# Queries' chain ahead of the first context's normalisation, and a last layer in one block

## The chip, the cores and the metric

One core of a Trainium2 chip runs the whole program. The metric is the device time of one execution in microseconds (us), median of several runs. All data are float32.

## What is computed

The reference is a stack of four levels, L0 to L3. Each level adds to the latents `x` (8 batches x 64 tokens x 256 features) a cross-attention with a context of 8 x 1601 tokens, a self-attention or state-space layer, and a feed-forward layer with experts. Each layer sees the layer-normalised `x`. Two of the twelve layers matter here.

The first, L0's cross-attention, with 16 heads of 64 features:

```
ctx' = layernorm(ctx) * ln_x_g + ln_x_b
lat  = layernorm(layernorm(x)) * ln_l_g + ln_l_b
q = rmsnorm(lat @ Wq) * qn_g ;  k, v = split([ctx'; lat] @ Wkv) ;  k = rmsnorm(k) * kn_g
x = x + softmax(q k' / 8 + mask) v @ Wout + bout
```

The last, L3's feed-forward layer, works on one normalised input z of 512 tokens x 256:

```
q, k, v = z @ W_qkv + b_qkv            # 16 heads of 16, 8 batches of 64 tokens
att = softmax(q k' / 4) v
gate = softmax(z @ W_gate + b_gate) ;  combine = the two largest of 8 entries, others 0
moe = sum over e of combine[:, e] * (z @ W_experts[e] + b_experts[e])
x = x + att + moe
```

The attention and the experts read the same z. Neither needs the other's result.

## The kernel before

The code issues every engine's instructions itself. An engine runs its own queue in order, and the queues meet only at semaphores. A layer is one block; `end_layer` (line 519) ends it with a barrier of all engines. `x` lives in SBUF as `L.x` (128 partitions, 4 tiles of 256), z as `L.z`, its transpose as `L.zT`. `program` (line 3932) loads x, constants and the first layer's weights on SyncE's queue (SP), then for each layer opens a small block in which SP issues the next layer's weights (lines 3954 to 3957), and then runs the layer. The weights alternate between `weights_a` and `weights_b`.

**L0's cross-attention (`l0_xattn`, line 770).** 64 steps, 8 batches x 8 head pairs. Ahead of the steps lie two preparations.

- The queries' chain. TensorE (PE) projects 8 parts with `project_q` (line 1262). ScalarE (ACT) squares each (1172), PE takes the mean per head with `mean_q` (1270), VectorE (DVE) clamps it (1005), ACT takes Ln and Exp (1163, 1165), and DVE multiplies (996, `q_gained`). With four PSUM banks, `project_q(p)` for p of 4 or more waits for the `q_gained(p - 4)` of four parts before, and `mean_q(p)` waits for the clamp of part p - 2.
- The first context. SP loads it into `keys_tok`. DVE takes statistics of two pieces of seven tiles each (`ctx_stats`: 950, 955, 958), ACT makes 1/std (`ctx_rstd`: 1156, 1158), DVE subtracts and multiplies tile by tile (`ctx_norm`: 965), and GpSimd (POOL) applies gain and bias for each piece (1126, 1128, `gains`), and then makes the mask row (1136).

DVE's queue has, in this order: both `ctx_stats`, both `ctx_norm`, and then the eight clamps with their gains. ACT's queue has both `ctx_rstd` ahead of its first square. PE's first work behind the queries, `turn_keys` (1296), waits for all eight queries, for POOL's last gain and bias, and for two copies of latents (`move_latents`). From there on the 64 steps follow.

**L3's last layer (`l3_ffn`, line 3809).** Two calls, two blocks. The first is `self_attention` (222). It normalises x, projects V (440) and Q, K (447), takes scores (457) and copies them out (325). Then come, for each of four tiles t: `shift` (329, 330), Exp on ACT (400), `divide` (336 to 338), a turn of the probabilities on PE (465, `turn_probs`), its copy by ACT (404), their product with V (476, `weigh`), `even_heads` on ACT (414), `attended` on DVE (345), a turn back (486, `project`) and `residual` (352). PE has dummy products in its gaps (`keep_busy`, 204). The second is `experts` (2625). Its logits (2845) go through `gate_vector` (2582 to 2622, a chain of small DVE operations with one Exp on ACT), two copies (2738, 2739), a turn of the combine matrix (2863) and its copy (2742). Then a loop over 8 experts:

```
pe.wait_ge(y_taken, e)      # PE: 16 products into the one pair of result banks (2901)
dve.wait_ge(y_done, e + 1)  # DVE: x += result * combine, four tiles (2774)
last.then_inc(y_taken, 1)
```

After the loop PE multiplies the biases (2913) and DVE adds them (2789). The last block stores x (3962).

## Time and profile before

| | before |
|---|---|
| median of 3 runs | 3238.86 us (3234.41 to 3239.84) |
| the profiled execution | 3242.19 us, of which the span from first to last instruction is 3240.4 us |
| granted TensorE clock, mean | 0.938 |
| instructions | 43628 |
| start of L0's step loop's preparation (`turn_keys`) | 69.73 us |
| last layer's first instruction to x's last addition | 3122.82 to 3235.93 us |

Times are those of one profiled execution, counted from its first instruction. The busy shares are averages over twelve layers with different limits, so the two places of the change are read on their own: us 0 to 70, and us 3122 to the end.

### The profile page before, as it was taken

What the parts mean: (1) busy time and instruction counts of PE and PEld (TensorE: products, weight loads), DVE (VectorE), ACT (ScalarE), POOL (GpSimd) and SP (SyncE); (2) the same over time, 40 slices, a digit from 0 to 9 for tenths busy, and PEclk for the clock granted to TensorE, in tenths of its full rate; (3) what the DMA queues carried; (4) which work ended last, traced back from release to release, by engine and by line L of the source; (5) the groups of instructions that cost most, each with busy time, mean ns of one, the idle gap of its engine ahead of it and who ended that gap; (6) DMA issues with size and microseconds to landing.
All of it is one profiled execution on the core that took longest, in us unless ns stands there. A gap on an engine that the chain in (4) does not pass through costs nothing. (4 is left out here: it accounts for less than half of the span.)

```text
span 3240.4 us, 43628 instructions
## 1 busy us (share of the span) xinstructions
PE 2822.7 (87%) x17456; PEld 1910.0 (59%) x17456; DVE 1634.3 (50%) x3626; ACT 1088.7 (34%) x1925; POOL 522.3 (16%) x280
## 2 busy tenths in 40 slices
PE   5899999999999998789999779989955789588776
PEld 2566666666666665446565536657932559477644
DVE  5556565665646454445555357754520520355463
ACT  2333333333333331135555446622311613111120
POOL 2012020211202000000000007731010320243200
PEclk8899999999999999889999989999977889799888
DMA  4123323232322210311000001126856158332101
GB/s 139 45 53 73 69 55 66 54 66 54 66 59 61 54 44 23 145 45 42 21 21 22 1 16 40 43 84 243 301 191 203 50 193 306 131 122 82 32 1 33
DMA packets 92096, 271.40 MB, mean 84 GB/s; under 512 B 7920, under 2 KB 57096, under 8 KB 85240
## 3 DMA queue, kind: packets, MB, share of 16 engines
q1 hardware_dynamic: 87896, 259.65, 26.6%
q0 software_dynamic: 2976, 8.13, 0.7%
q8 instruction: 138, 2.26, 0.3%
q10 hardware_dynamic: 1024, 0.86, 0.1%
q14 instruction: 62, 0.51, 0.1%
HBM read 256.64 MB, written 11.44 MB: 83 GB/s over the span
## 5 line engine op out<-in xcount | busy, mean ns | idle before, releaser
L1375 PE MATMUL L_xattn_bank<-L_xattn_keys_tok,L_xattn_probsT 119*128 119x257 f32 (+1 forms) x1792 | 452.7, 393 | 9.3 <-ACT L_xattn_probsT L1211 0.4
L1312 PE MATMUL L_xattn_wide<-L_xattn_keys_feat,weights_a 128*128 128x512 f32 (+2 forms) x1024 | 386.4, 521 | 1.3 <-DVE L_xattn_k_rnorm L1024 0.7
L1375 PEld LDWEIGHTS L_xattn_bank<-L_xattn_keys_tok,L_xattn_probsT 119*128 119x128 f32 (+1 forms) x1792 | 320.9, 190 | 96.5 <-issue 33.1
L1312 PEld LDWEIGHTS L_xattn_wide<-L_xattn_keys_feat,weights_a 128*128 128x128 f32 x1024 | 192.0, 193 | 153.8 <-issue 127.7
L1020 DVE COPY L_xattn_k_normed<-L_xattn_wide 128x833 f32<-128x833 f32 (+1 forms) x128 | 131.3, 1026 | 231.2 <-PE L_xattn_wide L1312 231.2
L2315 DVE TENSOR_TENSOR_SCAN L_attn_state<-L_attn_decay,L_attn_banks 128x1024 f32<-128x1024 f32 x80 | 182.7, 2286 | 69.6 <-PE L_attn_banks L2518 61.6
L1590 DVE CUSTOM_DVE_ANT_0 L_xattn_scores<-L_xattn_banks,L_xattn_mask 128x512 f32<-128x512 f32 (+1 forms) x256 | 131.4, 570 | 151.8 <-issue 151.8
L2421 POOL TENSOR_TENSOR L_attn_state<-L_attn_state,L_attn_C_rows 128x1024 f32<-128x1024 f32 x80 | 188.7, 2360 | 70.3 <-DVE L_attn_state L2315 70.2
L1126 POOL TENSOR_TENSOR L_xattn_keys_tok<-L_xattn_keys_tok,weights_a 119x1792 f32<-119x1792 f32 (+2 forms) x24 | 61.1, 2546 | 856.1 <-DVE L_xattn_keys_tok L965 856.1
L1205 ACT ACTIVATE L_xattn_scores<-L_xattn_scores,L_xattn_neg_max 128x833 f32<-128x833 f32 x128 | 119.6, 982 | 208.6 <-DVE L_xattn_neg_max L1045 208.6
L2518 PEld LDWEIGHTS L_attn_banks<-L_attn_B_diagonal,L_attn_dt_u_tok 128*128 128x128 f32 x1280 | 150.4, 193 | 66.3 <-issue 64.7
L1040 DVE CUSTOM_DVE_ANT_0 L_xattn_scores<-L_xattn_wide,L_xattn_mask_row 128x833 f32<-128x833 f32 x128 | 126.4, 1021 | 110.2 <-issue 110.2
L1656 ACT ACTIVATE L_xattn_probsT<-L_xattn_banks 128x512 f32<-128x512 f32 (+1 forms) x208 | 122.6, 597 | 163.7 <-PE L_xattn_banks L1728 163.7
L3407 PE MATMUL L_ffn_banks<-L_ffn_slot_features,L_ffn_expert_w 128*128 128x128 f32 x1440 | 169.1, 278 | 3.0 <-DVE x_tok L3237 3.0
L1211 ACT ACTIVATE L_xattn_probsT<-L_xattn_bank 119x512 f32<-119x512 f32 x128 | 76.4, 597 | 276.5 <-PE L_xattn_bank L1352 276.5
L2518 PE MATMUL L_attn_banks<-L_attn_B_diagonal,L_attn_dt_u_tok 128*128 128x128 f32 x1280 | 165.2, 283 | 3.9 <-ACT L_attn_B_diagonal L2377 3.9
L3407 PEld LDWEIGHTS L_ffn_banks<-L_ffn_slot_features,L_ffn_expert_w 128*128 128x128 f32 x1440 | 166.3, 195 | 3.8 <-DVE x_tok L3237 3.7
L1030 DVE TENSOR_TENSOR L_xattn_k_normed<-L_xattn_k_scale,L_xattn_k_normed 128x834 f32<-128x834 f32 x128 | 155.6, 1257 | 0.8 <-DMA L_xattn_k_scale<-L_xattn_k_scale_rows 0.8
L1728 PE MATMUL L_xattn_banks<-const,L_xattn_scores 128*128 128x128 f32 (+1 forms) x832 | 134.2, 288 | 24.7 <-DVE L_xattn_V L1581 10.7
L2056 PE MATMUL L_xattn_banks<-L_xattn_ctx_tok_and_one,L_xattn_k_tok 128*128 128x257 f32 (+1 forms) x416 | 108.5, 416 | 31.6 <-ACT L_xattn_k_by_ctx L2012 29.5
L1728 PEld LDWEIGHTS L_xattn_banks<-const,L_xattn_scores 128*128 128x128 f32 (+1 forms) x832 | 88.8, 142 | 79.3 <-issue 45.8
L1664 ACT ACTIVATE L_xattn_scores<-L_xattn_scores,L_xattn_neg_max 128x1601 f32<-128x1601 f32 x64 | 103.5, 1618 | 92.7 <-DVE L_xattn_neg_max L1593 92.7
(504 smaller groups left out, 4562.6 us busy)
## 6 DMA issues: line engine op xcount, KB each, us to landing
L_xattn_k_scale<-L_xattn_k_scale_rows SPq DMA_DIRECT2D x128, 417.0 KB, 5.1
L_xattn_ctx_feat<-in_ctx_feat SPq DMA_DIRECT2D x24, 1601.0 KB, 10.0
L_ffn_expert_w<-in_x_L_ffn SPq DMA_DIRECT2D x16, 2056.0 KB, 8.0
L_ffn_expert_w<-in_x_L_ffn SPq DMA_DIRECT2D x15, 1028.0 KB, 6.2
L_ffn_expert_w<-in_x_L_ffn SPq DMA_DIRECT2D x15, 1024.0 KB, 5.2
L_attn_C_rows<-L_attn_c_rows SPq DMA_DIRECT2D x48, 256.0 KB, 3.2
L_xattn_ctx_tok<-in_ctx_tok SPq DMA_DIRECT2D x8, 1536.0 KB
L_xattn_ctx_tok_and_one<-in_ctx_tok SPq DMA_DIRECT2D x8, 1536.0 KB
```

The lines of the kernel that those rows point to most:

```text
L1020: nc.vector.tensor_copy(kn[:, s % 2, a:a + n], ps).then_inc(k_copied, 1)
L1030: nc.vector.tensor_tensor(k, spread[:, 2 * x:2 * x + 2, :], k, ALU.mult).then_inc(kn_ready, 1)
L1040: nc.vector.tensor_tensor_reduce(sc2[:, h, 0:HALF], ps, mrow[b % 2][:, :], 1.0, -3.0e38, ALU.add, ALU.max, mx[:, h:h + 1]).then_inc(s_take ...
L1312: last = nc.tensor.matmul(wide[:, 2 * h + c, 0:n], wk[:, k, p * P:(p + 1) * P], xnT[b % 2][:, k, a:a + n], start=(k == 0), stop=(k == KT - 1))
L1375: last = nc.tensor.matmul(bS[:, 0:D + 1], pT[0:r, c, a, :, :].rearrange("p h q -> p (h q)"), xn[b % 2][0:r, t, :], start=(i == 0), stop=(i ...
L1590: nc.vector.tensor_tensor_reduce(sc[:, j, a:a + n], ps[:, j, 0:n], mk[:, a:a + n], 1.0, -3.0e38, ALU.add, ALU.max, mx[:, j, c:c + 1]).then ...
L1656: nc.scalar.activation(pT[0:r, i % RING, :, :], ps[0:r, 6 + n % 2, :].rearrange("p (a n) -> p a n", n=P), ACT.Copy).then_inc(pT_ready, 1)
L1728: last = nc.tensor.transpose(ps[0:r, 6 + n % 2, j * P:(j + 1) * P], sc[:, j, t * P:t * P + r], L.ident)
L2315: nc.vector.tensor_tensor_scan(h[:, p % RING, :, :].rearrange("p m n -> p (m n)"), dA[:, p % RING, :, :].rearrange("p m n -> p (m n)"), ba ...
L2421: nc.gpsimd.tensor_tensor(state, state, C[:, g % C_RING, :].unsqueeze(1) .broadcast_to([P, 2, N]), ALU.mult).then_inc(hC_ready, 1)
L2518: last = nc.tensor.matmul(banks[:, i + j, t * P:(t + 1) * P], duT[d][:, t, m * P:(m + 1) * P], diag[:, g % DIAG_RING, t, :], start=True, s ...
L3407: last = nc.tensor.matmul(bank[:, c, :], w1[:, k, f:f + P], xT[:, j % 2, k, :], start=(k == 0), stop=(k == KT - 1))
```

## The change

It has three parts.

1. In `l0_xattn` the queries' chain comes ahead on DVE and ACT. The two `ctx_stats` now stand behind the clamps and gains of parts 1 and 2, and the two `ctx_norm` behind those of parts 3 and 4. On ACT `ctx_rstd` stands behind parts 2 and 3.
2. The first layer has no small block ahead of it any more. SP issues the second layer's weights inside `l0_xattn`, behind the first context, its mask and both copies of latents, ahead of the second context.
3. `l3_ffn` calls one new function, `attention_and_experts`, in place of `self_attention` and `experts`. All eight experts' weights are loaded by two transfers at the layer's start. PE's dummy products are gone; the experts' products stand between the attention's steps, written out by hand. The results of an expert go to one of two pairs of banks, ACT scales them into `expert_out`, POOL adds them up in `experts_total`, and one addition on DVE adds the total to x at the end. The scores' four tiles share four banks, so the second pair of tiles is computed after the first pair has been copied out. The expert biases go into the bank of the attention's `project` as one more product. `experts` is deleted; nothing else called it.

The diff, cut to its core:

```
+def attention_and_experts(L, nc, w, w_ready, at):
...
+        def s_view(t):
+            c = (t % 2) * 256
+            return ps[:, 0:4, c:c + 256].rearrange("p j (a s) -> p j a s", s=S)
...
+        def o_view(t, h, k):
+            return ps[:, 2 * (t % 2):2 * (t % 2) + 2, (2 * h + k) * S:(2 * h + k + 1) * S]
+        def y_view(e):
+            return ps[:, 4 + 2 * (e % 2):6 + 2 * (e % 2), :].rearrange("p a (t n) -> p (a t) n", n=D)
+        with nc.Block() as block:
+            @block.sync
+            def _(sp):
+                for n in range(2):
+                    sp.dma_start(we[:, 4 * n:4 * n + 4, :], src[4 * n:4 * n + 4].rearrange("e p c -> p e c")
+                                 ).then_inc(experts_loaded[n], 16)
+            @block.vector
+            def _(dve):
...
+                norm_vector(L, dve, chain, ln_stats_ready, rstd_ready, z_ready)
...
+                    last = nc.vector.tensor_scalar(hb[:, m, :], hs[:, :], w[:, bq + m:bq + m + 1], None, ALU.mult)
+                chain(last)
+                nc.vector.tensor_copy(half[:, 0, 0, 0:2], hs[:, :]).then_inc(hs_ready, 1)
+                dve.wait_ge(zT_turned, 1)
+                nc.vector.tensor_copy(L.zT[:, 1, :], ps[:, 1, :]).then_inc(zT_ready, 1)
+                dve.wait_ge(logits_ready, 1)
+                gate_vector(L, nc, dve, chain, T, ps[:, 0, 0:NT * E], w[:, at["br"]:at["br"] + E], "top2", None,
+                            logits_taken, gate_exp_ready)
+                nc.vector.tensor_copy(half[:, 0, 0, 0:2], comb[:, 0, 0:2]).then_inc(comb_ready, 1)
+                dve.wait_ge(combT_turned, 1)
+                nc.vector.tensor_copy(combT[:, :, :], ps[0:E, 1, :].rearrange("p (t n) -> p t n", n=P)
+                                      ).then_inc(combT_ready, 1)
...
+                def residual(t):
+                    dve.wait_ge(projected, t + 1)
+                    nc.vector.tensor_tensor(L.x[:, t, :], L.x[:, t, :], ps[:, 2 * (t % 2), 0:D], ALU.add
+                                            ).then_inc(x_added, 1)
...
+                residual(3)
+                dve.wait_ge(x_added, NT)
+                dve.wait_ge(y_added, E)
+                chain(nc.vector.tensor_tensor(L.x[:, :, :], L.x[:, :, :], total[:, :, :], ALU.add))
+            @block.gpsimd
+            def _(pool):
+                for e in range(E):
+                    pool.wait_ge(y_scaled, e + 1)
+                    if e == 0:
+                        nc.gpsimd.tensor_copy(total[:, :, :], ys[0][:, :, :]).then_inc(y_added, 1)
+                    else:
+                        pool.wait_ge(y_added, e)
+                        nc.gpsimd.tensor_tensor(total[:, :, :], total[:, :, :], ys[e % 2][:, :, :], ALU.add).then_inc(y_added, 1)
+            @block.scalar
+            def _(act):
...
+                nc.scalar.activation(L.zT[:, 0, :], ps[:, 0, :], ACT.Copy).then_inc(zT_ready, 1)
+                act.wait_ge(logits_taken, 1)
...
+                def scale_expert(e):
+                    act.wait_ge(y_done, e + 1)
+                    if e == 0:
+                        act.wait_ge(comb_ready, 1)
+                    if e >= 2:
+                        act.wait_ge(y_added, e - 1)
+                    for t in range(NT):
+                        last = nc.scalar.activation(ys[e % 2][:, t, :], y_view(e)[:, t, :], ACT.Copy,
+                                                    scale=comb[:, t, e:e + 1])
+                    last.then_inc(y_scaled, 1)
+                scale_expert(0)
+                exponentials(0)
+                exponentials(1)
+                scale_expert(1)
+                scale_expert(2)
+                copy_turned(0)
+                exponentials(2)
+                even_heads(0)
+                copy_turned(1)
+                exponentials(3)
+                scale_expert(3)
+                even_heads(1)
+                scale_expert(4)
+                copy_turned(2)
+                scale_expert(5)
+                even_heads(2)
+                copy_turned(3)
+                scale_expert(6)
+                even_heads(3)
+                scale_expert(7)
+            @block.tensor
+            def _(pe):
...
+                pe.wait_ge(zT_ready, 2)
+                for t in range(NT):
+                    for k in range(KT):
+                        last = nc.tensor.matmul(ps[:, 0, t * E:(t + 1) * E], L.zT[:, k, t * P:(t + 1) * P],
+                                                wr[:, k, :], start=(k == 0), stop=(k == KT - 1))
+                last.then_inc(logits_ready, 1)
...
+                            for j in range(4):
...
+                def expert(e):
+                    pe.wait_ge(experts_loaded[e // 4], 16)
+                    if e >= 2:
+                        pe.wait_ge(y_scaled, e - 1)
+                    for t in range(NT):
+                        for k in range(KT):
+                            last = nc.tensor.matmul(y_view(e)[:, t, :], L.zT[:, k, t * P:(t + 1) * P],
+                                                    we[:, e, k * D:(k + 1) * D], start=(k == 0), stop=(k == KT - 1))
+                    last.then_inc(y_done, 1)
+                def turn_probs(t):
+                    pe.wait_ge(probs_ready, t + 1)
+                    if t >= 2:
+                        pe.wait_ge(x_added, t - 1)
+                    for n in range(8):
+                        b = 2 * (t % 2) + n // 4
+                        last = nc.tensor.transpose(ps[:, b, (n % 4) * P:(n % 4 + 1) * P],
+                                                   sc[t][:, 2 * n:2 * n + 2, :].rearrange("p b s -> p (b s)"), L.ident)
...
+                def project(t):
+                    pe.wait_ge(att_ready, KT * t + KT)
+                    out = ps[:, 2 * (t % 2), 0:D]
+                    nc.tensor.matmul(out, combT[:, t, :], b2, start=True, stop=False)
+                    for k in range(KT):
+                        last = nc.tensor.matmul(out[:, k * P:(k + 1) * P], aT[:, k, t * P:(t + 1) * P], L.ident,
+                                                start=False, stop=(k == KT - 1))
+                    last.then_inc(projected, 1)
+                project_qk(0)
+                pe.wait_ge(comb_ready, 1)
+                for t in range(NT):
+                    last = nc.tensor.transpose(ps[0:E, 1, t * P:(t + 1) * P], comb[:, t, :], L.ident)
+                last.then_inc(combT_turned, 1)
+                project_qk(1)
+                pe.wait_ge(v_ready, 1)
+                pe.wait_ge(combT_ready, 1)
+                pe.wait_ge(qk_act, 3)
+                pe.wait_ge(qk_dve, 3)
+                scores(0, 0)
+                scores(0, 1).then_inc(scored, 1)
+                expert(0)
+                pe.wait_ge(s_taken, 2)
+                scores(1, 0)
+                scores(1, 1).then_inc(scored, 1)
+                expert(1)
+                expert(2)
+                pe.wait_ge(s_taken, 4)
+                turn_probs(0)
+                expert(3)
+                turn_probs(1)
+                weigh(0)
+                expert(4)
+                weigh(1)
+                project(0)
+                expert(5)
+                project(1)
+                turn_probs(2)
+                expert(6)
+                turn_probs(3)
+                weigh(2)
+                expert(7)
+                weigh(3)
+                project(2)
...
@@ -928,6 +1303,7 @@
                 sp.wait_ge(latents_ready, 1)
                 for b in range(2):
                     move_latents(b)
+                L.load_next_weights(sp)
                 load_ctx(1)
                 load_mask(1)
                 for s in range(STEPS):
@@ -986,10 +1362,6 @@
                 nc.vector.memset(sq[:, KC:KP], 0.0).then_inc(mask_zeroed, 1)
                 dve.wait_ge(zT_turned, 1)
                 nc.vector.tensor_copy(L.zT[:, 1, :], wide[:, 1, :]).then_inc(zT_ready, 1)
-                for piece in range(2):
-                    ctx_stats(0, piece)
-                for piece in range(2):
-                    ctx_norm(0, piece)
 
                 def q_gained(p):
                     dve.wait_ge(q_rnorm, 2 * p + 2)
@@ -1005,6 +1377,10 @@
                     nc.vector.tensor_scalar(half, bank[:, :], 1e-16, None, ALU.max).then_inc(q_clamped, 1)
                     if p:
                         q_gained(p - 1)
+                    if p in (1, 2):
+                        ctx_stats(0, p - 1)
+                    if p in (3, 4):
+                        ctx_norm(0, p - 3)
                 q_gained(NQ - 1)
 
                 def keys_turned(b, k, x):
@@ -1163,8 +1539,6 @@
                     nc.scalar.activation(half, half, ACT.Ln).then_inc(q_rnorm, 1)
                     act.wait_ge(q_rnorm, 2 * p + 1)
                     nc.scalar.activation(half, half, ACT.Exp, scale=-0.5).then_inc(q_rnorm, 1)
-                ctx_rstd(0, 0)
-                ctx_rstd(0, 1)
                 for p in range(NQ):
                     act.wait_ge(q_projected, p + 1)
                     if p >= 2:
@@ -1173,6 +1547,8 @@
                                          ).then_inc(q_squared, 1)
                     if p:
                         q_rnormed(p - 1)
+                    if p in (2, 3):
+                        ctx_rstd(0, p - 2)
                 q_rnormed(NQ - 1)
 
                 def keys_turned(b, k, x):
@@ -2622,303 +2998,6 @@
         chain(nc.vector.tensor_tensor(comb[:, :, :], pr[:, :, :], oh[:, :, :], ALU.mult))
 
 
-def experts(L, nc, name, w, at, w_ready, kind, src, F, norm=True, swiglu=False, linear=False, sel_bias=False):
-    n_exp = src.shape[0]
-    cols = src.shape[2]
...
-    self_attention(L, nc, "L3_ffn_", w, [at[n] for n in ("Wq", "Wk", "Wv", "Wv")], HD ** -0.5,
-                   [at["bq"], at["bk"], at["bv"], None], None, True, w_ready)
-    experts(L, nc, "L3_moe_", w, at, w_ready, "top2", L.aps["x_L3_ffn"], D, norm=False, linear=True)
+    attention_and_experts(L, nc, w, w_ready, at)
 
 
 def expert_arrays(i, layers):
@@ -3950,11 +4027,15 @@
                 load_weights(sp, 0)
                 sp.wait_ge(x_loaded, 32)
         for n, (name, pack, run) in enumerate(packs):
-            if n + 1 < len(packs):
+            def load_next_weights(sp):
+                if n + 1 < len(packs):
+                    load_weights(sp, n + 1)
+            L.load_next_weights = load_next_weights
+            if name != "L0_xattn":
                 with nc.Block() as block:
                     @block.sync
                     def _(sp):
-                        load_weights(sp, n + 1)
```

## Rows read from the trace of the kernel before

**Rows 1.** The page, part 1: busy time, share of the span and instructions of each engine.

```profile
PE 2822.7 (87%) x17456; PEld 1910.0 (59%) x17456; DVE 1634.3 (50%) x3626; ACT 1088.7 (34%) x1925; POOL 522.3 (16%) x280
```

**Rows 2.** Timeline to 110 us: start, duration, engine, line, operation, count, [idle before, what ended it].

```profile
18.66 1.22 DVE L974 TENSOR_TENSOR z_tok<-z_tok,weights_a 128x1024 f32<-128x1024 f32 x1 [2.29 <-DMA weights_a<-in_w_L_xattn]
...
23.95 6.38 PE L1262 MATMUL L_xattn_wide<-z_feat,weights_a 128*128 128x512 f32 x8 [0.78 <-DVE z_feat L988]
...
30.98 2.38 DVE L950 BATCH_NORM_STATS2 L_xattn_ctx_stats<-L_xattn_keys_tok 119x6 f32<-119x256 f32 x7 [7.08 <-DMA L_xattn_keys_tok<-in_ctx_tok]
...
37.18 11.67 DVE L965 TENSOR_SCALAR L_xattn_keys_tok<-L_xattn_keys_tok,L_xattn_ctx_mean_var,L_xattn_ctx_rstd 119x256 f32<-119x256 f32 x14
...
39.70 3.85 POOL L1126 TENSOR_TENSOR L_xattn_keys_tok<-L_xattn_keys_tok,weights_a 119x1792 f32<-119x1792 f32 x1 [39.24 <-DVE L_xattn_keys_tok L965]
...
48.77 1.27 DVE L1005 TENSOR_SCALAR L_xattn_scores<-L_xattn_bank 128x512 f32<-128x512 f32 x2
...
56.10 0.72 POOL L1128 TENSOR_TENSOR L_xattn_keys_tok<-L_xattn_keys_tok,weights_a 54x256 f32<-54x256 f32 x1
...
60.88 0.74 DVE L996 SCALAR_TENSOR_TENSOR L_xattn_qT<-L_xattn_wide,L_xattn_q_gain,L_xattn_scores 128x512 f32<-128x512 f32 x1
...
69.73 2.73 PE L1296 MATMUL L_xattn_bank<-const,L_xattn_keys_tok 119*128 119x119 f32 x14 [3.20 <-DVE L_xattn_qT L996]
```

**Rows 3.** The lookup of line 965 in the first 60 us.

```profile
L965 DVE TENSOR_SCALAR L_xattn_keys_tok<-L_xattn_keys_tok,L_xattn_ctx_mean_var,L_xattn_ctx_rstd x14: 399/406/3940, 37.2 to 48.4; 119x256 f32<-119x256 f32 x13, 54x256 f32<-54x256 f32 x1
```

**Rows 4.** Windows: stretch, its length, busy us (count) of five engines, granted clock, DMA, GB/s.

```profile
56.60:69.70 13.10, 9.91 (x23) 3.95 (x21) 7.49 (x11) 8.35 (x14) 6.05 (x3) 1.00 0.04 8
...
3145.60:3149.10 3.50, 3.46 (x4) 1.45 (x5) 3.46 (x3) 1.06 (x1) 0.00 (x0) 0.52 0.02 5
...
3194.50:3232.60 38.10, 25.89 (x112) 20.70 (x112) 12.78 (x35) 0.00 (x0) 0.00 (x0) 1.00 0.15 41
```

**Rows 5.** Timeline of the last layer's attention, after us 3130.

```profile
3129.66 3.69 PE L440 MATMUL L_ffn_banks<-weights_b,z_feat 128*128 128x256 f32 x16 [0.87 <-DVE z_feat L299]
...
3133.19 7.03 PE L447 MATMUL L_ffn_banks<-z_feat,weights_b 128*128 128x512 f32 x16
...
3141.16 3.80 PE L457 MATMUL L_ffn_banks<-L_ffn_kT,L_ffn_q_of_head 32*128 32x64 f32 x128 [0.94 <-DVE L_ffn_kT L314]
...
3143.23 2.35 DVE L325 COPY L_ffn_scores<-L_ffn_banks 128x1024 f32<-128x1024 f32 x2 [2.22 <-PE L_ffn_banks L457]
...
3160.41 1.09 PE L465 MATMUL L_ffn_banks<-const,L_ffn_scores 128*128 128x128 f32 x8 [0.56 <-DVE L_ffn_scores L338]
...
3161.44 0.67 PE L476 MATMUL L_ffn_banks<-L_ffn_probsT,L_ffn_V 64*32 64x128 f32 x32
```

**Rows 6.** Timeline of the last layer's experts.

```profile
3178.08 3.55 PE L2845 MATMUL L_moe_bank<-weights_b,z_feat 128*128 128x8 f32 x16 [1.77 <-PEq L522]
...
3185.67 0.17 DVE L2739 COPY L_moe_combine_e<-L_moe_combine 128x4 f32<-128x4 f32 x1
...
3196.20 3.72 PE L2901 MATMUL L_moe_bank<-L_moe_expert_w,z_feat 128*128 128x256 f32 x16 [1.75 <-DVE x_tok L2774]
...
3234.71 1.22 DVE L2789 TENSOR_TENSOR x_tok<-x_tok,L_moe_wide 128x1024 f32<-128x1024 f32 x1 [0.26 <-PE L_moe_wide L2913]
```

**Rows 7.** Groups by line and shape, 3116 to 3241: busy us, mean ns, idle before.

```profile
L330 DVE TENSOR_TENSOR L_ffn_scores<-L_ffn_scores,L_ffn_max 128x1024 f32<-128x1024 f32 x4 | 4.9, 1224 | 0.1
...
L336 DVE TENSOR_REDUCE L_ffn_sum<-L_ffn_scores 128x16 f32<-128x1024 f32 x4 | 4.8, 1208 | 0.0
...
L404 ACT ACTIVATE L_ffn_probsT<-L_ffn_banks 128x1024 f32<-128x1024 f32 x4 | 4.1, 1022 | 9.2 <-PE L_ffn_banks L465 9.2
...
L414 ACT ACTIVATE L_ffn_even_heads_out<-L_ffn_banks,weights_b,const 128x128 f32<-128x128 f32 x8 | 3.2, 454 | 5.5 <-PE L_ffn_banks L476 5.5
```

**Rows 8.** Lookups of lines 2421 and 3285: their instructions over the whole run.

```profile
L2421 POOL TENSOR_TENSOR L_attn_state<-L_attn_state,L_attn_C_rows x80: 2341/2360/2374, 1950.7 to 2601.9; 128x1024 f32<-128x1024 f32 x80
...
L3285 ACT ACTIVATE L_ffn_slot_out<-L_ffn_banks x30: 364/383/384, 2237.4 to 2764.7; 128x256 f32<-128x256 f32 x30
```

460 lines of the change are left out of this document (190 added, 270 removed).

## The prediction

> **What bounds the kernel now.** The page's first part comes first: PE is busy 87% of the span, DVE 50%, ACT 34%, POOL 16% [rows 1]. Those are averages over twelve layers. The change touches two places only, so I read each in the timeline. In the first 70 us PE stands idle for long: it projects two parts of the queries until 30.3, and then nothing moves in their chain, because DVE waits for the context to land (30.98), takes its statistics, and normalises fourteen tiles until 48.85. The first clamps run at 48.77, and the turns of the keys start at 69.73, released by the last query [rows 2]. POOL had finished the context at 56.8 [rows 2], so the queries' chain set that start. At the other end, the attention's PE has dummy products in its gaps, and each expert is a strict alternation: 3.72 us of PE, then 1.75 us in which PE waits for DVE's addition into x [rows 6]. One expert costs 5.47, seven of them 38.3, and in that stretch PE is busy 68% at full clock, DVE a third, ACT and POOL not at all [rows 4]. The two parts of one layer, which share only z, run one behind the other.
>
> **The removed small block and the moved weights: nothing.** DVE can start about 0.8 us earlier, but then it waits for the first layer's weights anyway: it idled 2.29 us for them before line 974 [rows 2]. That wait is the cover; it only grows. On SP the second layer's weights are moved past the first context, its mask and two copies of latents, and stand ahead of the second context. The first context may land earlier than 30.98, but DVE now wants it only at 35. The second context is wanted in step 1, behind the turns at 69.7 [rows 2], tens of us after its issue. If that cover were gone, the cost would be the 1.2 MB's own time, some 3 us; I put it into the range.
>
> **The queries' chain ahead: 5 us.** I lay the queues out from the rows. PE ends the first two projections at 30.3, as now. The clock is then full, if PE stays busy: a record of 512 columns takes 9.91 / 23 = 0.43 us at clock 1.00 [rows 4]. The first mean (two records) ends at 31.2, the next projection and mean (six) at 33.8. DVE's clamp takes 1.27 / 2 = 0.64 and its gain 0.74 [rows 2], so clamp 1 and gain 0 end at 35.2. A piece of statistics costs (37.18 - 30.98) / 2 = 3.1 [rows 2]: 38.3. Clamp and gain: 39.7. Second piece: 42.8. Clamp and gain: 44.2. Seven normalisations take 39.70 - 37.18 = 2.5 [rows 2]: 46.7. Meanwhile PE waits for clamps a few times, but has enough parts ahead. From here POOL is late: from its start to its last bias it took 56.82 - 39.70 = 17.1 [rows 2], so the context is ready at 63.9. The queries end earlier. The second seven normalisations stand behind POOL's first two operations (7.6 us) as they do now, until about 55.9; three clamps and four gains with ACT's steps between need 6.4 more: 62.3. What is late next is thus POOL, not the queries. The turns start at 64.0 in place of 69.7. PE comes to them out of an idle stretch, and the first eight, which now run at full clock, will take about 0.5 more. Net 5 us, passed on to the end, since the steps behind are a chain that starts there. Bounds: 0, if the clock stays at half in the chain (48 records at 6.38 / 8 = 0.80 and more [rows 2] end near 65, with DVE's and ACT's tail near 68, and POOL near 69.5), and 8, if POOL is not held up at all.
>
> **The last layer in one block: 39 us.** Both versions are alike up to 3129.63, when `z_feat` is there; the old one ends at 3234.71 + 1.22 = 3235.93 [rows 5, 6]: 106.3 us. In the new one I add up PE's queue at full clock. Logits: 3.55 at half clock [rows 6], so 1.8. V 3.6 and Q, K 7.0 [rows 5]. The turn of `combine`: 0.55, an estimate from eight turns in 1.09 [rows 5]; its input is ready, since the gate's chain, 3185.84 - 3181.63 = 4.2 [rows 6], runs under V and the first half of Q, K. Then a wait of 0.85 for DVE's last key copy. Scores 3.8 [rows 5]. Eight experts at 3.72: 29.8 [rows 6]. Four turns at 1.09 and four products with V at 0.67: 7.0 [rows 5]. Two of the attention's projections, 0.7 each with the bias product (an estimate: two turns are 0.27 [rows 5], the bias and fill the rest): 1.4. Together 55.0 of work and 0.85 of waiting.
>
> DVE decides in the middle. From the first scores' end (3145.4) it copies two tiles (2.35 [rows 5]), makes two shifts (each 1.21 + 1.22 [rows 7]), copies two more (2.35) and divides one (1.21 + 1.22 [rows 7] and a short reciprocal, 0.25 as an estimate, a little above line 2739's 0.17 [rows 6]): to 3157.9, while PE, after experts 0 to 2, wants it at 3158.5. That would fit. But POOL's additions come in between. At line 965 one tile took 3940 ns against a median of 406 [rows 3]: it stood through POOL's 3.85 us operation of line 1126 [rows 2]. DVE's operations of lines 330 and 338 have all inputs in SBUF, like that one, and POOL's addition is of the size of line 2421, 2.36 us [rows 8]. Two additions fall into that stretch; they delay DVE by 1.8 + 1.4, and a later one by 1.1, so PE waits 2.6 us ahead of the first turn and 1.5 ahead of the second. Afterwards PE is behind everything else and runs without gaps.
>
> The Trainium skill (SBUF — State Buffer, Who interferes with whom) says that VectorE and GpSimd share a port pair as an exclusive lock, held for a whole instruction, and that a VectorE instruction with two SBUF inputs takes part in it. That speaks against additions on GpSimd here. With the rule the block takes 66.3 us, without it 62.2; the trace agrees with its whole-instruction part (3940 ns, rows 3).
>
> PE's last product with V thus ends 55.0 + 0.85 + 4.1 = 60.0 us after 3129.63. Then the tail, which nothing hides: `even_heads` 0.81 (4 x 0.81 = 3.2 [rows 7]), four scaled copies of expert 7 on ACT, POOL's addition 2.36, DVE's 1.22 [rows 6], and three hand-overs of 0.05. A scaled copy of 256 columns is not in the trace. The nearest is line 3285 of the same shape, 383 ns without a scale column [rows 8]; line 414 takes 454 ns for 128 columns with scale and bias columns [rows 7], 570 if the further 128 columns cost as in line 404 (1022 ns for 1024 [rows 7]). I take 0.44, nearer to the first, so 1.75 for four, bounds 1.5 and 2.3. The tail is 6.3. Total 66.3, against 106.3: 40.0 saved. I take off 1 for one stretch at half clock: the clock fell to 0.52 behind the 3.8 us of small score products, though PE was busy [rows 4], and the new code has such products too, now followed by experts. The first such stretch (1.75 us lost) lies under the DVE wait, a later one counts. 39 us; bounds 28 (a third of the block at half clock, below) and 44 (no contention).
>
> **The sum.** 5 + 39 = 44. The profiled execution took 3242.19, 1.8 around its span, and lies 3.3 above the median of the runs, within what one run differs from another; it would become 3198. The median, 3238.86, becomes 3194.9: I say 3195.
>
> **Rivals.** (a) No contention. Speaks for it: POOL's additions may fall between DVE's. Without the 4.1 us of waits the block takes 62.2 and saves 44, L0 6 to 8: 3188. (b) The queries' chain gives nothing, because the clock falls to half in it; for it: the present chain starts at half clock after each idle stretch. Against it: it was full at 56.6 to 69.7 with PE busy 76% [rows 4]. 3238.9 - 39 = 3200. (c) The clock falls in the last block, as it did at 3145.6 [rows 4], now without the dummy products. With a third of PE's work at half clock the block takes 55 x 4/3 + 7.2 = 80.5 (DVE's waits vanish in it), saves 26, and the run is 3208; with half of it 3217. Against it: the old loop of experts held clock 1.00 with PE busy 68% [rows 4], and the new block is denser. (d) Slower: PE stays at half clock all through the block, since nothing keeps it busy through the waits for DVE. Then the block takes 2 x 55 + 7.2 = 117.3, 11 more than now, L0 gives nothing, and the run is 3250. It decides from a factor of 1.92 on PE's work: practically the whole block at half.
>
> **How the numbers follow.** What differs from no change by less than 0.2%, 6.5 us, can't be told from it. The forecast (3190.5 to 3199) gets 0.60, (a) 0.10, (b) 0.12, (c) 0.14, within 0.2% 0.02, (d) and slower 0.02. The range takes in (a), (b) and the first half of (c), with the unknown prices: 3186 to 3212, and leaves out some 1 in 10, less than I might, because hand-laid queues tend to miss small waits. Faster 0.96, same 0.02, slower 0.02.
>
> **What the profile after would show.** Line 965's first seven tiles end near 46.7, the turns start near 64, released by POOL's last bias and no longer by the last query. The new layer's last addition ends 66 us after `z_feat`, PE is busy over 85% in it at clock near 1, and POOL has eight additions of 2.4 us. DVE's line 330 or 338 operations show single durations well over 1.22 where POOL runs. The prediction is wrong if the clock in the block is under 0.9, if the turns are still released by the last query, or if steps of the first layer behind the turns change their length.

## The result and the profile after

| | median us | runs | ratio to before [interval] |
|---|---|---|---|
| before | 3239.35 | 3234.41 to 3240.38 | |
| after | 3198.21 | 3195.70 to 3204.97 | 0.9879 [0.9861, 0.9898] |
| after, with new runs of both | 3196.5 | 3195.32 to 3203.56 | 0.9868 [0.9849, 0.9887] |

The changed kernel is faster by 41 us; 44 were forecast (3195.0, and 3186 to 3212). Its profiled execution took 3195.7 us, with a span of 3193.9, against the 3240.4 of before. The page's part 1, which answers to [rows 1]:

```profile
PE 2798.0 (88%) x17448; PEld 1897.8 (59%) x17448; DVE 1623.4 (51%) x3585; ACT 1100.6 (34%) x1957; POOL 539.4 (17%) x288
```

PE's busy share is nearly the same (87% before), while its busy time fell by 24.7 us: the dummy products went, and so did idle gaps. POOL has 17 us more.

**Where the 46.5 us between the two spans came from.** Each layer's first BATCH_NORM_STATS2 marks its start. The second layer starts at 1250.37 instead of 1259.95, which is 9.6 earlier; the last layer at 3116.62 instead of 3122.85, 6.2 earlier, so that 3.4 were lost in layers that nobody changed; the rest, 40.3, came in the last layer. Its block took from `z_feat` to the end of the last addition 3189.26 - 3123.18 = 66.1 us, where before took 3235.93 - 3129.63 = 106.3 [rows 5, 6].

**The first layer.** Timeline of the changed kernel, 22 to 90 us: start, duration, engine, line, operation, count, and in brackets the idle time before and what ended it.

```profile
31.39 0.69 DVE L1377 TENSOR_SCALAR L_xattn_scores<-L_xattn_bank 128x512 f32<-128x512 f32 x1 [7.22 <-PE L_xattn_bank L1646]
...
43.96 2.34 DVE L1341 TENSOR_SCALAR L_xattn_keys_tok<-L_xattn_keys_tok,L_xattn_ctx_mean_var,L_xattn_ctx_rstd 119x256 f32<-119x256 f32 x7
...
46.48 3.71 POOL L1502 TENSOR_TENSOR L_xattn_keys_tok<-L_xattn_keys_tok,weights_a 119x1792 f32<-119x1792 f32 x1 [46.02 <-DVE L_xattn_keys_tok L1341]
...
47.48 8.26 DVE L1341 TENSOR_SCALAR L_xattn_keys_tok<-L_xattn_keys_tok,L_xattn_ctx_mean_var,L_xattn_ctx_rstd 119x256 f32<-119x256 f32 x7
...
58.20 2.08 PE L1646 MATMUL L_xattn_bank<-L_xattn_k_square,const 128*128 128x512 f32 x2 [7.74 <-ACT L_xattn_k_square L1546]
...
62.37 0.75 DVE L1368 SCALAR_TENSOR_TENSOR L_xattn_qT<-L_xattn_wide,L_xattn_q_gain,L_xattn_scores 128x512 f32<-128x512 f32 x1 [0.70 <-ACT L_xattn_scores L1541]
62.97 0.71 POOL L1504 TENSOR_TENSOR L_xattn_keys_tok<-L_xattn_keys_tok,weights_a 54x256 f32<-54x256 f32 x1
...
63.79 3.23 PE L1672 MATMUL L_xattn_bank<-const,L_xattn_keys_tok 119*128 119x119 f32 x14 [3.51 <-DVE L_xattn_qT L1368]
...
69.98 5.83 PE L1688 MATMUL L_xattn_wide<-L_xattn_keys_feat,weights_a 128*128 128x512 f32 x16 [0.59 <-DVE L_xattn_keys_feat L1391]
```

The first clamp ran at 48.77 before [rows 2], and runs at 31.39 now. DVE normalises seven tiles (2.34 us) and POOL starts at once. The next seven take 8.26 us, because they stand behind POOL's first two operations, as in [rows 3]; that is also why PE stands idle for 7.74 us ahead of its means at 58.20. The last query ends at 62.37 + 0.75 = 63.12, POOL's last bias at 62.97 + 0.71 = 63.68, and the turns start at 63.79, against 69.73 [rows 2]. The profile names DVE as the releaser, but POOL's bias came last, by 0.56 us.

**The last block.** Timeline of the changed kernel.

```profile
3123.18 1.92 PE L786 MATMUL L_ffn_banks<-weights_b,z_feat 128*128 128x8 f32 x16 [0.88 <-DVE z_feat L628]
...
3124.96 5.39 PE L791 MATMUL L_ffn_banks<-weights_b,z_feat 128*128 128x256 f32 x16
...
3145.92 1.03 POOL L706 COPY L_ffn_experts_total<-L_ffn_expert_out 128x1024 f32<-128x1024 f32 x1 [113.44 <-ACT L_ffn_expert_out L753]
...
3151.53 2.34 POOL L709 TENSOR_TENSOR L_ffn_experts_total<-L_ffn_experts_total,L_ffn_expert_out 128x1024 f32<-128x1024 f32 x1 [4.57 <-ACT L_ffn_expert_out L753]
3151.75 3.21 DVE L661 TENSOR_TENSOR L_ffn_scores<-L_ffn_scores,L_ffn_sum 128x1024 f32<-128x1024 f32 x1
...
3154.98 2.37 POOL L709 TENSOR_TENSOR L_ffn_experts_total<-L_ffn_experts_total,L_ffn_expert_out 128x1024 f32<-128x1024 f32 x1 [1.11 <-ACT L_ffn_expert_out L753]
...
3155.10 1.06 PE L830 MATMUL L_ffn_banks<-const,L_ffn_scores 128*128 128x128 f32 x8 [1.80 <-DVE L_ffn_scores L661]
...
3156.11 2.31 DVE L653 TENSOR_TENSOR L_ffn_scores<-L_ffn_scores,L_ffn_max 128x1024 f32<-128x1024 f32 x1
...
3161.16 1.09 PE L830 MATMUL L_ffn_banks<-const,L_ffn_scores 128*128 128x128 f32 x8 [1.54 <-DVE L_ffn_scores L661]
...
3185.58 2.34 POOL L709 TENSOR_TENSOR L_ffn_experts_total<-L_ffn_experts_total,L_ffn_expert_out 128x1024 f32<-128x1024 f32 x1 [0.99 <-ACT L_ffn_expert_out L753]
...
3188.03 1.23 DVE L699 TENSOR_TENSOR x_tok<-x_tok,L_ffn_experts_total 128x1024 f32<-128x1024 f32 x1 [0.81 <-POOL L_ffn_experts_total L709]
```

Line 661 is the old line 338, line 653 the old 330, which took 1.22 us each [rows 7]. Line 661 started at 3151.75, 0.22 behind a POOL addition (3151.53), and took 3.21; line 653 took 2.31 beside the next. PE stood idle for 1.80 us ahead of turn 0 of the probabilities (3155.10), and 1.54 ahead of turn 1. The tail is there too: POOL's last addition, then DVE's.

Windows of the changed kernel: stretch, its length, busy us (count) of PE, weight loads, DVE, ACT, POOL, granted clock, DMA share, GB/s.

```profile
3123.18:3125.00 1.82, 1.82 (x17) 1.82 (x17) 0.00 (x0) 0.00 (x0) 0.00 (x0) 1.00 0.45 171
3125.00:3128.00 3.00, 3.00 (x9) 2.42 (x10) 2.32 (x19) 0.23 (x1) 0.00 (x0) 0.55 0.00 0
...
3130.00:3141.00 11.00, 10.06 (x88) 5.63 (x87) 3.30 (x5) 3.15 (x4) 0.00 (x0) 1.00 0.01 2
3141.00:3157.00 16.00, 14.20 (x125) 12.22 (x124) 15.83 (x13) 7.50 (x15) 5.40 (x3) 1.00 0.00 1
3157.00:3170.00 13.00, 11.46 (x116) 9.01 (x115) 11.56 (x15) 7.67 (x16) 3.05 (x3) 1.00 0.01 1
3170.00:3180.00 10.00, 10.00 (x85) 8.22 (x84) 3.61 (x5) 3.49 (x8) 4.37 (x2) 1.00 0.01 2
...
3123.18:3189.26 66.08, 58.28 (x492) 44.90 (x492) 40.59 (x65) 26.47 (x53) 17.51 (x8) 0.96 0.02 6
```

From 3130 to 3180 PE is busy 45.7 of 50 us at clock 1.00, and the clock of the whole block is 0.96. The stretch that costs something is V's: the logits ran at 1.00, then the clock is 0.55 from 3125 to 3128 although PE is busy without a gap, and V took 5.39 us (3124.96 above), where before took 3.69 [rows 5].

### The profile page after: what moved, and what is told of

Read it like the earlier page. It is cut to its first block and busy times, and to the rows that moved or that the text cites. A ratio compares the mean times of both kernels' runs of the same rounds, so it can differ in the third digit from the quotient of the medians.

```text
span 3193.9 us, 43529 instructions
## 1 busy us (share of the span) xinstructions
PE 2798.0 (88%) x17448; PEld 1897.8 (59%) x17448; DVE 1623.4 (51%) x3585; ACT 1100.6 (34%) x1957; POOL 539.4 (17%) x288
## 3 DMA queue, kind: packets, MB, share of 16 engines
q10 hardware_dynamic: 1024, 0.86, 0.1%
## 5 line engine op out<-in xcount | busy, mean ns | idle before, releaser
L2894 PEld LDWEIGHTS L_attn_banks<-L_attn_B_diagonal,L_attn_dt_u_tok 128*128 128x128 f32 x1280 | 150.3, 193 | 66.3 <-issue 64.7
L2104 PE MATMUL L_xattn_banks<-const,L_xattn_scores 128*128 128x128 f32 (+1 forms) x832 | 134.3, 288 | 24.7 <-DVE L_xattn_V L1957 10.7
L2432 PE MATMUL L_xattn_banks<-L_xattn_ctx_tok_and_one,L_xattn_k_tok 128*128 128x257 f32 (+1 forms) x416 | 108.7, 417 | 31.6 <-ACT L_xattn_k_by_ctx L2388 29.5
```

The lines of the kernel that those rows point to most:

```text
L2104: last = nc.tensor.transpose(ps[0:r, 6 + n % 2, j * P:(j + 1) * P], sc[:, j, t * P:t * P + r], L.ident)
L2894: last = nc.tensor.matmul(banks[:, i + j, t * P:(t + 1) * P], duT[d][:, t, m * P:(m + 1) * P], diag[:, g % DIAG_RING, t, :], start=True, s ...
```

## Experiments

The kernels ran in four series, each with runs of the kernel before on the same chip: its medians were 3242.69 us (19 runs; parts alone, additions without reads), 3239.8 (7 runs; the next four), 3240.63 (9 runs; the changed kernel again, three edits) and 3240.88 (15 runs; the last two). Ratios are to the runs of the same series.

### Each part of the change alone

**The queries' chain only**, in the kernel before:

```diff
-                for piece in range(2):
-                    ctx_stats(0, piece)
-                for piece in range(2):
-                    ctx_norm(0, piece)
...
+                    if p in (1, 2):
+                        ctx_stats(0, p - 1)
+                    if p in (3, 4):
+                        ctx_norm(0, p - 3)
...
-                ctx_rstd(0, 0)
-                ctx_rstd(0, 1)
...
+                    if p in (2, 3):
+                        ctx_rstd(0, p - 2)
```

> The kernel before with the first change alone: in the first layer the queries' chain ahead of the context's statistics and normalisation on DVE and ACT. Theory: this part carries its share by itself. The turns of the keys start near 64 in place of 69.7 us, the first keys after them run at full clock, and the 64 steps end 8 to 10 us earlier; the time falls by 6 to 9 us. Rival (the prediction's own size): the steps only inherit the 5 us, and the rest of what the first layer gained came from elsewhere; the time falls by 5.

Measured: 3232.87 (10 runs), ratio 0.9974 [0.9963, 0.9985]. Its timeline:

```profile
23.99 5.16 PE L1262 MATMUL L_xattn_wide<-z_feat,weights_a 128*128 128x512 f32 x8 [0.78 <-DVE z_feat L988]
...
62.46 3.22 PE L1296 MATMUL L_xattn_bank<-const,L_xattn_keys_tok 119*128 119x119 f32 x14 [3.52 <-DVE L_xattn_qT L992]
```

The turns start 7.3 us earlier than at 69.73: the new order, and on top of it the first projections ran more of their time at full clock (5.16 us for eight records against 6.38 [rows 2]). The first layer took 1240.2 us against 1251.4, a pair of profiles that flatters it (below). The ratio says 8 us, and its interval, 5 to 12, holds both the theory's 6 to 9 and the rival's 5, so this run shows that the new order gains and doesn't decide between them.

**The last layer only**, in the kernel before; the first layer and the weights' loads are the old ones:

```diff
 def l3_ffn(...)
-    self_attention(...)
-    experts(...)
+    attention_and_experts(L, nc, w, w_ready, at)
```

> The kernel before with the last layer in one block alone. Theory: the time from z_feat to the last addition is 66 us in place of 106, as in the changed kernel, and the whole run falls by 40. The rival says that the parts are not additive (for example a clock state inherited from the layers before): more than 3 us off from 40.

Measured: 3200.86 (4 runs), ratio 0.987 [0.9853, 0.9886]; the block took 3198.46 - 3132.4 = 66.1 us, as in the changed kernel. This part carries nearly all of the result. The theory's 40 is met: the runs fell by 42.

**The weights' loads only**, behind the first context instead of in a small block of their own:

```diff
+                L.load_next_weights(sp)      # in l0_xattn, SP's queue
...
-            if n + 1 < len(packs):           # the small block ahead of the layer
+            if name != "L0_xattn":
```

> The kernel before with the first small block removed and the second layer's weights issued behind the latents' copies, nothing else. Theory: the first context lands several us earlier, DVE's statistics in the old order start earlier than 30.98 by 3 to 5 us, and since the old chain hangs on them, the turns start 3 to 5 us earlier here, though this part is worth nothing in the changed kernel, where DVE comes to the statistics at 35. Rival: the landing is not what DVE waited for, and the start stays at 69.7.

Measured: 3238.58 (10 runs), ratio 0.9988 [0.9979, 0.9998]. The context's statistics start at 27.22 us instead of 30.98 and the turns at 65.88 instead of 69.73. In the kernel before, DVE waited for that transfer, and all behind it comes 3.8 us earlier, as the theory had it; against the second profile of before (below), whose statistics start at 30.05 and turns at 68.25, it is 2.4. I had this part at nothing. In the changed kernel DVE takes the statistics at 35.23 without any wait for a DMA, and so it does with the order alone (33.89). The two parts don't add up: the order alone brings the turns to 62.46, both together to 63.79, and to 62.74 in a second profile of the changed kernel. Whether the moved weights cost something there was not measured: the order alone is the earliest of all, with one profile.

### What the last block is made of

**POOL's additions without their reads.** The changed kernel with seven additions replaced; the experts' sum is left out of the output:

```diff
-                        nc.gpsimd.tensor_tensor(total[:, :, :], total[:, :, :], ys[e % 2][:, :, :], ALU.add).then_inc(y_added, 1)
+                        nc.gpsimd.memset(total[:, :, :], 0.0).then_inc(y_added, 1)
```

> The changed kernel; POOL's seven additions of expert results are replaced by fills of the same tile with zeros, which read nothing, so the experts' sum is left out of the result. Theory of contention: DVE's subtraction and division beside POOL, up to 3.2 us each, all take 1.22 us, and PE's two waits ahead of the turns of tiles 0 and 1 (1.8 and 1.5 us) nearly go; the fill is also shorter than the addition by about 1.3 us in the tail: 4 to 5 us less in all, of which 1.3 in the tail. Rival: the waits come from DVE's own queue; they stay, and only the tail's 1.3 us go.

Measured: 3191.31 (4 runs), ratio 0.9846 [0.983, 0.9863]; the block took 3182.42 - 3119.97 = 62.45 us, 3.6 less. The lookup of line 661 (count, minimum, median and maximum in ns, first and last start), and lines of the timeline:

```profile
L661 DVE TENSOR_TENSOR L_ffn_scores<-L_ffn_scores,L_ffn_sum x4: 1224/1224/1225, 3148.5 to 3164.2; 128x1024 f32<-128x1024 f32 x4
```

```profile
3142.71 1.03 POOL L706 COPY L_ffn_experts_total<-L_ffn_expert_out 128x1024 f32<-128x1024 f32 x1 [113.44 <-ACT L_ffn_expert_out L753]
...
3143.35 1.47 DVE L653 TENSOR_TENSOR L_ffn_scores<-L_ffn_scores,L_ffn_max 128x1024 f32<-128x1024 f32 x1
...
3148.30 0.95 POOL L709 MEMSET L_ffn_experts_total<- 128x1024 f32 x1 [4.55 <-ACT L_ffn_expert_out L753]
3148.54 1.22 DVE L661 TENSOR_TENSOR L_ffn_scores<-L_ffn_scores,L_ffn_sum 128x1024 f32<-128x1024 f32 x1
...
3154.88 1.09 PE L830 MATMUL L_ffn_banks<-const,L_ffn_scores 128*128 128x128 f32 x8 [0.46 <-DVE L_ffn_scores L661]
```

With POOL at 0.95 us and without inputs, all four of line 661 take 1224 ns, where they took 1224 to 3205. The wait ahead of turn 0 is gone, and that of turn 1 fell from 1.54 to 0.46. So the long DVE operations were made long by POOL, and the waits of PE followed from them. The memset is also shorter than the addition, but that is not what did it: line 661 started at 3148.54, 0.24 behind a memset that ran until 3149.25, and still took 1.22. The copy of line 706, which reads, is left in this kernel; line 653, begun 0.39 ahead of its end, took 1.47 in place of 1.22, as in the changed kernel. Of the 3.6 us, 3.1 lie ahead of the end of PE's last product with V (56.9 us behind the block's start instead of 59.95) and 0.6 in the tail, where PE's last steps now come last and not POOL. That is a little under the 4 to 5 expected, of which 1.3 were to lie in the tail.

**V ahead of the logits**, in the changed kernel: the two loops of products change places.

> The changed kernel, with the products of V ahead of the gate's logits on PE; everything else the same. In the changed kernel the products of V, behind the logits, took 5.39 us instead of 3.69 before. Theory: the logits' products, 8 columns each, are what brings the clock down; V ahead of them takes 3.6 to 3.7 us and the block from z_feat to the last addition is up to 1.7 us shorter (64.4 in place of 66.1), if the clock does not fall behind the logits instead. Rival: the fall only moves, to the products of Q and K behind the logits; then the block keeps its 66.

Measured: 3194.93 (1 run, so it is read by its profile only). Timeline, first products of the block:

```profile
3123.40 3.69 PE L786 MATMUL L_ffn_banks<-weights_b,z_feat 128*128 128x256 f32 x16 [0.87 <-DVE z_feat L628]
...
3126.93 1.85 PE L792 MATMUL L_ffn_banks<-weights_b,z_feat 128*128 128x8 f32 x16
...
3128.63 3.68 PE L799 MATMUL L_ffn_banks<-z_feat,weights_b 128*128 128x512 f32 x8
...
3132.84 0.60 PE L858 MATMUL L_ffn_banks<-const,L_ffn_combine 128*8 128x128 f32 x4 [0.53 <-DVE L_ffn_even_heads_out L633]
```

V takes 3.69 us again, and the logits 1.85. The slow stretch did not move elsewhere: Q and K's first half, right behind the same logits, takes 3.68. So the logits' narrow products don't slow what follows them wherever they stand. In the changed kernel they stand right behind PE's wait of 0.88 us for `z_feat`; whether it takes that wait too was not tested. Of the 1.7 us, 0.7 are given back, mostly as a wait of 0.53 for the gate's result, which now comes later. The block took 65.1 us, 1.0 less, between the 64.4 of the theory and the rival's 66.

**The last expert added by DVE**, straight from PSUM, in the changed kernel:

```diff
+                for t in range(NT):
+                    last = nc.vector.scalar_tensor_tensor(L.x[:, t, :], y_view(E - 1)[:, t, :], comb[:, t, E - 1:E],
+                                                          L.x[:, t, :], ALU.mult, ALU.add)
...
-                for e in range(E):           # POOL
+                for e in range(E - 1):
```

> The changed kernel; the last expert's result goes from its banks straight into x by four operations on DVE, in a stretch where DVE waits, and the total of the other seven is added to x ahead of the last tile's residual. Theory: the tail behind PE's last product is ACT's four scaled copies, POOL's addition and DVE's, and with this edit the attention's own last steps are what ends last: the last operation on x ends about 2 us earlier (64.1 in place of 66.1 us behind z_feat). Rival: DVE is too late with the four operations and holds up the attention's last tile; 66 or more.

Measured: 3196.81 (1 run, read by its profile only); the block took 3190.37 - 3126.18 = 64.2 us, 1.9 less and as expected (64.1): ACT's four copies and POOL's addition have left the tail.

**Is it the overlap?** The changed kernel with all eight experts behind the whole attention, in the same block:

```diff
-                expert(0)                    # and 1 to 7, between the attention's steps
...
+                for e in range(E):           # behind project(3)
+                    expert(e)
```

> The changed kernel; the eight experts stand behind the whole attention on PE and on ACT, in the same block, with the same buffers and without dummy products. Theory: half of the block's gain is the overlap of the attention's waits with experts, the other half the experts' own loop without DVE in it. The block takes 51 us for the attention (the 47.1 of before, and logits, the turn of combine and the clock), 29.8 for the experts and 5.2 of tail: 86 us in place of 66, against 106 before. The rival on the clock says more: without experts between its steps and without dummy products PE's clock falls to half in the attention, and the block takes over 92.

Measured: 3221.25 (4 runs), ratio 0.9939 [0.9922, 0.9955]. The block took 3214.63 - 3123.02 = 91.6 us, between the two expectations. Its windows and its first turn:

```profile
3142.00:3150.00 8.00, 3.69 (x64) 3.50 (x64) 7.93 (x8) 2.11 (x2) 0.00 (x0) 0.52 0.01 2
3150.00:3160.00 10.00, 4.25 (x32) 3.55 (x40) 9.79 (x10) 1.97 (x2) 0.00 (x0) 0.50 0.00 0
3160.00:3170.00 10.00, 8.12 (x86) 5.76 (x66) 7.12 (x13) 3.47 (x6) 0.00 (x0) 0.50 0.00 0
```

```profile
3152.71 1.94 PE L824 MATMUL L_ffn_banks<-const,L_ffn_scores 128*128 128x128 f32 x8 [6.11 <-DVE L_ffn_scores L661]
```

PE is busy 46%, 43% and 81% in these stretches at a clock of 0.50 to 0.52, and a turn takes 1.94 us instead of 1.06. The overlap, with the clock that it keeps up, is worth 91.6 - 66.1 = 25.5 of the 40 us. In the other 14.7 stands the loop of the experts: two pairs of result banks, with ACT taking the results instead of DVE, 29.5 us for the eight experts where the old loop took 8 x 5.47 = 43.8 [rows 6], so 14.3. (An expert is 8 products in the code, and 16 records in the trace.) The start of a layer that is saved besides, and the half clock here, were not measured apart from it.

I tried to part the clock's share from that of the filled gaps, with 37 dummy products in the gaps of that kernel.

> The run before with the experts behind the whole attention in one block took 91.6 us for the block, and TensorE was at half clock in the attention (four turns of the probabilities 1.9 us instead of 1.1). Here the same order, with 37 dummy products of TensorE put into the attention's gaps, so that the clock stays up. It parts the two gains of the overlap: the filled gaps themselves, and the clock that a filled TensorE keeps. By the theory that both count, the turns take 1.09 us again, the steps on the attention's chain are shorter by some 5 us in all (scores 1.7, turns 0.85 each for those on the chain, products with V 0.44 each, projections 0.5 each), and the block takes about 86 us; the filled gaps are then worth 20 us of the 25.5 and the clock 5. By the rival that the attention's chain is DVE's and ACT's and the clock doesn't matter to it, the block stays at 91 us or more, since dummies that are too many would only delay the turns.

Measured: 3227.37 (6 runs), ratio 0.9961 [0.9944, 0.9978]; block 3219.24 - 3120.94 = 98.3 us, 6.7 more. This doesn't answer the question. Its timeline:

```profile
3144.72 10.57 PE L204 MATMUL L_ffn_banks<-const 128*128 128x512 f32 x24
...
3149.27 1.22 DVE L661 TENSOR_TENSOR L_ffn_scores<-L_ffn_scores,L_ffn_sum 128x1024 f32<-128x1024 f32 x1
...
3155.13 1.04 PE L824 MATMUL L_ffn_banks<-const,L_ffn_scores 128*128 128x128 f32 x8
```

The clock was 1.00 from 3130 on and the turns took 1.04 us, as wanted. But the probabilities of tile 0 were ready at 3149.27 + 1.22 = 3150.5, and 12 dummies in a row held PE until 3155.1. I had sized a dummy as one record of 0.43 us, and it is two (24 records for 12 in the line above), so each dose was twice what the gap held. The theory's 86 us is missed. The number lies where the rival put it, at 91 or more, and by the reason that the rival names for too many dummies, but that says nothing on the rival's own claim, that the clock doesn't matter. One part of the clock's share can be read: the eight experts behind the attention took 27.79 us here and 29.48 in the run before, so 1.7. How much of the remaining 25.5 us is the clock stays open.

### The start of the first layer

**The context earlier.** The changed kernel with both statistics ahead of the chain and all fourteen tiles normalised together behind the second clamp; POOL waits for all of them:

```diff
+                for piece in range(2):
+                    ctx_stats(0, piece)
...
-                    if p in (1, 2):
-                        ctx_stats(0, p - 1)
-                    if p in (3, 4):
-                        ctx_norm(0, p - 3)
+                    if p == 1:
+                        ctx_norm(0, 0)
+                        ctx_norm(0, 1)
...
-                    pool.wait_ge(ctx_normed, 2 * b + n + 1)
+                    pool.wait_ge(ctx_normed, 2 if b == 0 else 2 * b + n + 1)
```

> The changed kernel; in the first layer both pieces' statistics stand ahead of the queries' chain on DVE, both pieces' normalisations together behind the second clamp, and POOL starts only when both pieces are normalised. Theory: with the weights moved the first context lands near 27 us, DVE is idle there, and POOL's work, which sets the start of the keys' turns, starts near 41 in place of 46.5 and no longer stands in the way of DVE's normalisation: the turns start near 57 in place of 63.8, and the run is 6 to 8 us shorter than the changed kernel. Rival: the queries' chain is what the turns wait for (the profile's row names it); then the start moves by less than 3 us.

Measured: 3190.46 (3186.38 to 3192.02, 4 runs), ratio 0.9848 [0.9831, 0.9864].

```profile
36.43 4.60 DVE L1341 TENSOR_SCALAR L_xattn_keys_tok<-L_xattn_keys_tok,L_xattn_ctx_mean_var,L_xattn_ctx_rstd 119x256 f32<-119x256 f32 x14
...
41.21 3.71 POOL L1504 TENSOR_TENSOR L_xattn_keys_tok<-L_xattn_keys_tok,weights_a 119x1792 f32<-119x1792 f32 x1 [40.75 <-DVE L_xattn_keys_tok L1341]
...
55.84 0.71 POOL L1506 TENSOR_TENSOR L_xattn_keys_tok<-L_xattn_keys_tok,weights_a 54x256 f32<-54x256 f32 x1
...
56.65 3.23 PE L1675 MATMUL L_xattn_bank<-const,L_xattn_keys_tok 119*128 119x119 f32 x14 [5.18 <-issue]
```

The fourteen tiles take 4.60 us instead of 2.34 + 8.26, since POOL isn't at work yet. POOL runs from 41.21 to 56.55 in one go, and the turns start at 56.65, 7.1 us earlier, where 57 were expected. It shows which queue sets the start: POOL's end moved from 63.68 to 56.55, also 7.1, while the last query's moved from 63.12 to 54.6, which is 8.5.

### Both kernels again, and the sum of the good edits

**The changed kernel again**, with no edit:

> The changed kernel itself, once more, so that the next kernel is read against it on one chip. Expected 3198 us within 3, the turns of the first layer's queries at 63.8 us from the span's start, the block of the last layer 66.1 us from its first product to its last addition. In the stretch of the third layer's cross-attention the profile of the changed kernel took 3.4 us more than that of the kernel before with the same instructions: by the theory that this is the run's and not the change's, it falls somewhere between 137 and 140.5 us here; by the rival that the change causes it, it is within 0.5 us of 140.4 again.

Measured: 3196.5, block 66.1 us, turns at 62.74 (expected 63.8), and 137.0 us for the cross-attention of the third level (L2), as in the kernel before.

**The kernel before again**, with no edit:

> The kernel before, once more with its profile. Six kernels with the changed kernel's first layer took 1242.5 to 1245.8 us for that layer, three with the old order of its queries' chain 1245.3 to 1251.4 (one of them with the weights moved). By the theory that the change gives the first layer some 6 us, and that the 8.8 us between the two profiles of before and after are partly the run's own, this run's first layer falls between 1247 and 1252, and its turns of the keys start at 69 to 70 us from the span's start. By the rival that the whole 8.8 us are the change's, it takes 1251 or more.

Measured: 3240.88 (10 runs), ratio 1.0 [0.9989, 1.0012]. Its first layer took 1247.0 us, at the lower edge of what the theory allows, under the rival's 1251, and 4.4 less than in the first profile of the same code. Turns at 68.25, under the 69 to 70 expected. Its timeline, and the window from 70 to 80 us of the first profile of before and of this one:

```profile
68.25 3.25 PE L1296 MATMUL L_xattn_bank<-const,L_xattn_keys_tok 119*128 119x119 f32 x14 [3.21 <-DVE L_xattn_qT L996]
...
74.47 5.83 PE L1312 MATMUL L_xattn_wide<-L_xattn_keys_feat,weights_a 128*128 128x512 f32 x16 [0.59 <-DVE L_xattn_keys_feat L1015]
```

```profile
70.00:80.00 10.00, 9.15 (x32) 5.63 (x31) 2.12 (x4) 2.27 (x4) 0.00 (x0) 0.52 0.01 2
```

```profile
70.00:80.00 10.00, 8.98 (x37) 5.30 (x36) 3.15 (x5) 2.60 (x4) 0.00 (x0) 0.92 0.01 2
```

The first products of the keys took 7.81 us in the first profile of before and 5.83 here, with the same instructions: the clock was 0.52 in the one and 0.92 in the other.

**Three edits together**: V ahead of the logits, the last expert on DVE, the context earlier.

> The changed kernel with three edits together: V's products ahead of the logits' in the last block (alone 1.0 us there), the last expert added to x by VectorE instead of GpSimd (alone 1.9 us), and the first layer's context normalised as one piece ahead of the queries (alone 7.1 us at the turns). By the theory that each acts on a place of its own they add up: block 66.1 - 1.0 - 1.9 = 63.2 us, turns of the queries at 56.7 us, and 10 us less in all, 3188 us against 3198 for the changed kernel. By the rival that the first two share a wait (the weights of the turns come from VectorE's queue, where the last expert now stands as well), the block stays over 64.2 us. By the rival that the 7 us of the first layer are given back in the later stages, the run is at 3194 or more.

Measured: 3184.61 (3181.4 to 3186.2, 5 runs), ratio 0.9824 [0.981, 0.9839]: 12 us less than the changed kernel in the same series. The turns start at 56.51 (expected 56.7), and the block took 3178.17 - 3114.97 = 63.2 us (expected 63.2), so that both rivals, over 64.2 us and 3194 or more, are refuted. Its end:

```profile
3173.05 2.36 POOL L716 TENSOR_TENSOR L_ffn_experts_total<-L_ffn_experts_total,L_ffn_expert_out 128x1024 f32<-128x1024 f32 x1 [3.34 <-ACT L_ffn_expert_out L760]
...
3173.45 1.66 DVE L697 SCALAR_TENSOR_TENSOR x_tok<-L_ffn_banks,L_ffn_combine,x_tok 128x256 f32<-128x256 f32 x4 [2.21 <-PE L_ffn_banks L826]
...
3176.17 1.21 DVE L704 TENSOR_TENSOR x_tok<-x_tok,L_ffn_experts_total 128x1024 f32<-128x1024 f32 x1
...
3177.75 0.42 DVE L675 TENSOR_TENSOR x_tok<-x_tok,L_ffn_banks 128x256 f32<-128x256 f32 x1 [0.37 <-PE L_ffn_banks L857]
```

POOL's last addition and DVE's last expert now lie under PE's last products, and the last instruction is a residual of 0.42 us.

## Why the prediction held, and where it was off

**The last layer: 39 to 40 us forecast, 40.2 measured.** The block was laid out at 66.3 us and took 66.1 in three executions. Its terms, those of PE from the start of one step to the start of the next:

| term | forecast | measured |
|---|---|---|
| wait ahead of turn 0 and turn 1 | 2.6 + 1.5 | 1.80 + 1.54 |
| logits, to V's start | 1.8 | 1.78 |
| V, to Q's start | 3.6 | 5.22 |
| eight experts | 29.8 | 28.8 |
| four turns, four products with V | 7.0 | 6.2 |
| two projections with their bias product | 1.4 | 2.3 |
| four scaled copies | 1.75 | 1.57 |
| POOL's addition | 2.36 | 2.34 |
| a stretch at half clock | 1, late in the block | 1.6, in V's term |

With the 1 us for the clock the forecast was 67.3, and 1.2 more than measured: the waits were 0.8 too long, the experts 1.0, the turns and products with V 0.8 and the copies 0.2, against which the projections cost 0.9 more and the clock 0.6 more than laid out. That the 66.3 of the layout lies so near the 66.1 is in part luck: terms that were 2.8 too long stand against 1.6 of clock and 0.9 of projections. The projections' 0.7 each was an estimate, and it is 1.17 (3167.03 to 3168.20). The clock's place was wrong too. I put the slow stretch behind the scores; it fell behind the logits, whose products are only 8 columns wide. With V first it is gone, though the logits are still there. The contention was the step that could have failed most, and the run without POOL's reads shows it: the two waits fell from 3.34 to 0.46 us, by 2.9, where 4.1 was forecast. The Trainium skill (SBUF — State Buffer, Who interferes with whom) gives the rule of the exclusive lock; by its whole-instruction part line 661, begun 0.22 us behind an addition of 2.34, takes 2.34 - 0.22 + 1.22 = 3.34, and it took 3.21.

**The first layer: 5 us forecast, 5.9 handed on.** Seven tiles normalised by 46.7, it was 46.30; the second seven by 55.9, it was 55.74; last query 62.3, it was 63.12; POOL's last bias 63.9, it was 63.68; turns 64.0, it was 63.79. That POOL and no longer the queries would set the start holds by 0.56 us only, and the earlier context shows it plainly, since the turns moved by as much as POOL's end did. The page's releaser says the opposite, since it names the last query.

The first pair of profiles gives the layer 9.6 us, nearly twice the forecast. That was not the change's doing. The length of the layer in the profiles of these experiments:

| first layer | lengths in us |
|---|---|
| old order (before, before again, last layer only) | 1251.4, 1247.0, 1247.6 |
| new order (changed, changed again, and five with its first layer) | 1242.6, 1244.3, 1242.9, 1242.8, 1245.8, 1242.5, 1243.8 |
| new order, weights where they were | 1240.2 |
| old order, weights moved | 1245.3 |

The means of the first two rows are 1248.7 and 1243.5, 5.1 us apart; 0.8 come on top, as the layer starts that much earlier without the small block. That is 5.9 in all, but the three of the old order are 4.4 apart, so it is good to a few us only. The medians of the runs don't resolve it either: the last layer alone is at 0.987 [0.9853, 0.9886], the whole change at 0.9868 [0.9849, 0.9887] in its new runs. The keys' first products at full clock, which I first took for a gain handed on by the change, are found with the old order too. My last sentence of what would make the prediction wrong, that steps behind the turns change their length, was met by the first profile, and it took a second profile of before to see that the length changes by itself.

**The layers behind: 0 forecast, -3.4 in the first pair.** The third level's cross-attention took 137.0 us before and 140.4 after. In the twelve later profiles it took 136.7 to 139.8, and in the changed kernel's second one 137.0. All the layers between the first and the last took 1862.9 us in the first profile of before, 1865.3 in its second, and 1862.8 to 1871.6 in the rest, so the loss isn't the change's.

**The removed block and the moved weights: 0 forecast.** Nothing contradicts it for the changed kernel, and it is wrong as a statement about the edit: alone, it gives the turns 2.4 to 3.8 us. I had named the cover, that DVE wants the context only at 35, and it holds only with the other edit.

**The rivals.** No contention (3188) is refuted by the 3.21 us of line 661. That the queries' chain gives nothing (3200) is near the median too; what refutes it is the run with the chain alone, 0.9974 [0.9963, 0.9985]. The clock in the last block was 0.96, which refutes both a third of it at half clock (3208) and the slower rival, half clock all through. The median lies 3.2 above the forecast, within what the runs of one kernel differ.

## What to carry to other kernels

Lay the queues of all engines out step by step from rows and ask which comes last after the edit: here that found POOL behind the queries, and a further 7 us lay in finishing DVE's normalisation before POOL was at work. Two edits that remove the same wait don't add up, so price each with the other in place. Before a difference of 5 us in one stage of one pair of profiles is explained, look at a second profile of the kernel before.

## What the runs showed of the hardware

- The clock can fall while PE is busy without a gap. With the logits first (8 products of 8 columns in 16 records, 1.92 us), V behind them took 5.38 or 5.39 us in all eight profiles with that order, with a clock of 0.55 over 3 us of it. With V first, in two profiles, it took 3.69, the logits 1.85, and what stood behind the logits was not slowed.
- With the same code, PE's clock in one stretch of 10 us was 0.52 in one execution and 0.92 in another, and from the turns' start to the first copy of the keys 81.63 - 69.73 = 11.9 us passed in the one, 77.54 - 68.25 = 9.3 in the other.
- A DVE operation of 1.22 us took 3.21 beside one POOL addition of 2.34, and seven of 2.34 us in all took 8.26 beside two of 3.71 and 3.70. With memsets on POOL (0.95 us, no input) all four were 1.22, one of them begun 0.24 us behind a memset; beside POOL's copy of 1.03 us, which reads, one took 1.47.
- POOL's copy of 1024 columns took 1.03 us, its memset 0.95, its addition of two such tiles 2.34. A scaled copy of 256 columns from PSUM on ACT took 1.57 / 4 = 0.39.
